# Routed feed-forward on one core: the transposes of the products moved behind the down projection

## What is computed

```python
x = x + attention(layernorm(x))            # degree-4 polynomial attention
x = x + ffn(layernorm(x))                  # routed feed-forward
x = x + silu(convolution(layernorm(x)))    # over the tokens, few taps matter
x = x + ffn(layernorm(x))                  # the same weights again

def ffn(x):   # 16 experts of width 176, 6 for a token; a shared one of width 352
    shared = (silu(x @ sg.T) * (x @ su.T)) @ shared_w2.T
    p = softmax(x @ gate_w.T); w, chosen = top_k(p, 6)
    return shared + sum(w[e] * ((silu(x @ w1g[e].T) * (x @ w1u[e].T)) @ w2[e].T) for e in chosen)
```

## Time and profile before

| | |
|---|---|
| median of 3 runs | 2374.47 us (2369.16 to 2383.44) |
| time of the profiled execution | 2393.97 us |
| its span in the trace | 2392.2 us |
| busy: PE, DVE, ACT, POOL | 2024.0, 1398.8, 1202.7, 1098.4 us |
| granted TensorE clock, mean | 0.907 of full speed |
| attention | about the first 720 us of the span |
| feed-forward and the rest | about 748 to 2320 us of the span |

### The profile page before, as it was taken

How to read it: one execution, slowest core, us unless ns; L and a number is a source line. 1 busy time by engine, 2 the same in 40 slices (tenths; PEclk the granted TensorE clock), 3 DMA queues, 4 the chain that set the end, 5 groups by cost and what they waited for, 6 DMA issues and landing times.

```text
span 2392.2 us, 42920 instructions
## 1 busy us (share of the span) xinstructions
PE 2024.0 (85%) x11630; PEld 1384.2 (58%) x11630; DVE 1398.8 (58%) x4050; ACT 1202.7 (50%) x2924; POOL 1098.4 (46%) x1235
## 2 busy tenths in 40 slices
PE   5678998998886786999988989988888999999970
PEld 3334444544434564777766767756556777677650
DVE  3556777766875664433478543587775336634643
ACT  2446665655753453455544545545444555455440
POOL 1324444444661167772453057553557717205616
PEclk8778898889878898999999999999989999999995
DMA  3174466422406433564663246653534647537743
GB/s 101 32 192 98 141 184 173 93 79 52 88 10 154 133 117 136 202 222 153 190 192 105 83 158 222 213 175 122 154 133 170 217 151 235 179 120 218 228 137 108
DMA packets 266875, 350.91 MB, mean 147 GB/s; under 512 B 55456, under 2 KB 234976, under 8 KB 265952
## 3 DMA queue, kind: packets, MB, share of 16 engines
q1 hardware_dynamic: 229792, 247.46, 36.0%
q0 software_dynamic: 36864, 100.71, 12.9%
HBM read 189.42 MB, written 167.64 MB: 149 GB/s over the span
## 4 chain that ended last, share of the span: by engine, by line
PE 42%; DVE 17%; issue 4%; POOL 4%; ACT 2%; SPq 1%; DMA 1%; POOLq 0%; DVEq 0%; ACTq 0%
PE ffn_psum L1433 22%; PE ffn_psum L1461 11%; PE ffn_psum L1441 5%; PE ffn_psum L1409 4%; DVE acc L1313 3%; DVE ysh_sb L1313 3%; POOL rows L1084 2%; POOL xs L1070 2%; DVE ac L1231 2%; DVE al L1235 1%; DVE ac L1230 1%; ACT sg L1108 1%; DVE f_stats L1205 1%; DVE xn L1326 1%; DVE lag L1325 1%
## 5 line engine op out<-in xcount | busy, mean ns | idle before, releaser
L1433 PE MATMUL ffn_psum<-w,xt 128*128 (+1 forms) x2152 | 750.8, 471 | 19.6 <-issue 19.5
L1084 POOL DMA_INDIRECT rows<-ys,idx x384 | 375.9, 979 | 418.4 <-DMA ys<-yo 286.0
L1230 DVE TENSOR_TENSOR ac<-sg,ffn_psum 128x64 f32<-128x64 f32 x602 | 130.4, 217 | 590.2 <-ACT sg L1108 587.3
L1108 ACT ACTIVATE sg<-ffn_psum 128x176 f32<-128x176 f32 x602 | 191.2, 318 | 560.2 <-PE ffn_psum L1433 560.2
L1433 PEld LDWEIGHTS ffn_psum<-w,xt 128*128 128x128 f32 x2152 | 377.3, 194 | 153.4 <-issue 39.7
L1461 PE MATMUL ffn_psum<-wd,ah 128*128 (+1 forms) x1806 | 446.3, 316 | 0.2 <-DVE al L1235 0.2
L440 DVE TENSOR_TENSOR a<-a 128x1024 f32<-128x1024 f32 (+2 forms) x304 | 326.1, 1097 | 125.3 <-ACT a L343 124.8
L343 ACT ACTIVATE a<-attn_psum 128x1024 f32<-128x1024 f32 (+1 forms) x320 | 290.8, 941 | 161.2 <-PE attn_psum L654 160.8
L1070 POOL DMA_INDIRECT xs<-xn,idx x288 | 282.9, 982 | 156.4 <-issue 86.2
L1441 PEld LDWEIGHTS ffn_psum<-f_ident,ac 128*128 128x128 f32 x1204 | 164.9, 144 | 308.7 <-DVE ac L1231 173.5
L1441 PE MATMUL ffn_psum<-f_ident,ac 128*128 128x128 f32 x1204 | 242.5, 284 | 113.9 <-DVE ac L1231 113.7
(11 more groups left out here) (178 smaller groups left out, 2363.7 us busy)
## 6 DMA issues: line engine op xcount, KB each, us to landing
xin<-xs SPq DMA_DIRECT2D x474, 128.0 KB
ys<-yo SPq DMA_DIRECT2D x474, 128.0 KB
acc<-x SPq DMA_DIRECT2D x24, 512.0 KB, 4.6
xs<-x SPq DMA_DIRECT2D x3, 2944.0 KB, 12.2
qt<-sq SPq DMA_DIRECT2D x128, 64.0 KB, 2.3
kt<-sq SPq DMA_DIRECT2D x128, 64.0 KB, 2.3
ysh<-yo SPq DMA_DIRECT2D x64, 128.0 KB
ysh_sb<-ysh SPq DMA_DIRECT2D x16, 512.0 KB, 6.0
```

The source lines that it names most:

```text
L1084: pool.indirect_dma_start(rowset(q, b)[:, k, :], None, ys[g % 3][0:NBK[g] * P, :], bass.IndirectOffsetOnAxis(at, 0)).then_inc(s_rows[j % 4 ...
L1108: act.activation(sg[:, n % 2], GU(n)[:, 0:IH], ACT.Silu).then_inc(s["sg"], 1)
L1433: last = pe.matmul(GU(n)[:, 0:wide], x[:, k * P:(k + 1) * P], of(k), start=k == 0, stop=k == KE - 1)
```

## The change

On PE, `transpose_act(n-1)` moves from behind `gate_up(n)` to the end of the round, behind `down(n-2)`. On ACT, `high_act(n-1)` moves from behind `silu(n)` to behind `output(n-2)`, so that ACT meets the PE steps in the new order. Nothing is added or removed; DVE, POOL and SP keep their lists. The line numbers below are those of the kernel before, which the order of the calls alone changes.

```diff
@@ ACT
                 if 0 <= n < NI:
                     silu(n)
-                if 0 <= n - 1 < NI:
-                    high_act(n - 1)
                 if 0 <= n + 2 < NI and own_x(n + 2):
                     high(n + 2)
...
                 if 0 <= n - 2 < NI and closes(n - 2):
                     output(n - 2)
+                if 0 <= n - 1 < NI:
+                    high_act(n - 1)
@@ PE
                 if 0 <= n < NI:
                     gate_up(n)
-                if 0 <= n - 1 < NI:
-                    transpose_act(n - 1)
                 if 0 <= n + 2 < NI and own_x(n + 2):
                     transpose_rows(n + 2)
                 if 0 <= n - 2 < NI:
                     down(n - 2)
+                if 0 <= n - 1 < NI:
+                    transpose_act(n - 1)
```

## The result

| | before | after |
|---|---|---|
| median | 2378.09 us (4 runs, 2369.16 to 2383.44) | 2502.18 us (4 runs, 2494.55 to 2511.72) |
| profiled execution, its span | 2393.97, 2392.2 us | 2503.97, 2502.2 us |
| granted TensorE clock, mean | 0.907 | 0.920 |

The ratio is 1.0528 (95% interval 1.0476 to 1.0579): slower by 5.3%, 124 us by the medians and 110 us by the two spans. The forecast was 2522 us.

The account below looks back on a forecast made before the run. PE bounds the kernel, its steps back to back at 2.22 us a routed round. The terms 95 + 4 + 43 + 5 = 147 us, added to 2374.5, gave 2522 us; 2440 to 2575 for 8 in 10, own range 2480 to 2565.

Parts of the forecast that it names:

- step 2: DVE's other work starts 0.79 us later: +4 us for 22 `add_rows`, +43 us for 78 other waits.
- Step 1, the ring: Routed rounds: `gate_up` through late `al` and PE's sequencer to a later `gate_up`; 2.42 us for 2.22, +95 us.
- the extra step: PE's sequencer: one more register step for the waits of `transpose_act`, 0.15 us in the two-round path.
- the 0.10 of the sum: PE, routed rounds: a `gate_up` whose weights come late loses 0.10 us in the two-round path.
- The 0.64 us of room: Undisturbed routed round before the change: `al` plus sequencer take 3.80 us, the `gate_up` behind starts at 4.44.
- ring is dearer: Rival: slow TENSOR_LOADs decide, or the clock falls in longer rounds; 2.57 us a round, 2592 us, chance 0.10.
- ring is hidden: Rival: PE's sequencer gets ahead of the wait, rounds stay at 2.22; +80, so 2455 us, chance 0.20.
- "+43": 78 waits near shared items, each priced at 0.55 us, the middle between 0.20 and 0.91; bounds 16 and 71 us.
- Step 3, the removed wait: PE: the 113.7 us of `transpose_act` waits for the product nearly vanish but aren't gained; `down` meets the same delay.
- Step 4, the clock: PE's granted clock: longer waits in dense stretches may bring a few more drops, +5 us, between 0 and 25.
- The signs asked for: Traces: 2.42 us rounds, "issue" before `gate_up` some hundreds of times, `down` waiting for `al`, `al` at 3.31 to 3.33 us.
- faster: Rival: short product waits vanish with the "issue" behind them; up to 133 us gained, half expected, 2314 us, chance 0.04.

Follow-up runs that it names:

- the early read: Read of the expert's number moved one round earlier, ahead of the wait for `al`: kernel before 2348.15 us, changed kernel 2423.69 us.
- a second read: Expert's number read twice for each routed item: changed kernel 3265.3 us, ratio 1.0721; kernel before 3141.56 us, ratio 1.033.
- ACT's half: Kernel before with only `high_act(n-1)` moved behind `output(n-2)`, PE's order kept: 3120.28 us, ratio 1.0335, and 2512.75 us, ratio 1.0559.
- the transposes in the middle: Kernel before with `transpose_act(n-1)` between `transpose_rows(n+2)` and `down(n-2)`, `high_act(n-1)` between `high(n+2)` and `output`: 2385.57 us, ratio 1.0024.
- the undisturbed comparison: Follow-up runs with their own runs of the kernel before, which took 2380.45 us (13 runs), as in the result.
- the long one: Follow-up runs in which engines stood still for 1 to 50 us at a time; the kernel before took 3011.05 us, in another such set 3041.77 us.

## Why the prediction came out right, and where it was off

Slower was right, and so was the main mechanism; the amount was 2522 against 2502 us, inside the range. That it came so near is in part luck: the price of a ring round was too low, and the rounds that pay it and the price of step 2 were too high.

**Step 1, the ring.** Shown. The best of the rounds came as it was worked out: `high_act` 0.29 behind `output` (0.29), `al` at 3.31 (3.33), `al` to the next load 1.39 and 1.43 (1.41 with the extra step). The `gate_up` of that 3.31 had its weights in time and took 1.35 us; where they come late it takes 1.45, and `al` comes at 3.41, as in 69 of the 91 rounds. So the 0.10 of the sum was right as well. But the windows give 2.47 us a round, not 2.42. Most of the difference is that I took a median where a ring pays for every slow read. Over the 91 clean rounds the reads are (ns min/median/max), in the changed kernel and then in the one before:

```profile
L1423 PEldq TENSOR_LOAD <-table x91: 295/307/762, 979.8 to 1202.5; - x91
```

```profile
L1423 PEldq TENSOR_LOAD <-table x91: 296/302/537, 979.4 to 1179.7; - x91
```

By the records of each round the mean of a read in the changed kernel is 0.38 us, one in eight is over 0.60, and from the end of `al` to the second `gate_up` it is 1.56 us on the mean (1.39 to 1.91); `al` itself comes at 3.39 on the mean (3.31 to 3.42). 3.39 + 1.56 = 4.95 for two rounds, 2.47 for one. Of the 0.21 over the best rounds' 4.74, the reads themselves are 0.08, the later `al` 0.08 (the late weights, which the sum had), and the rest comes behind the read. Before, the reads were quicker (0.32 on the mean, none over 0.54) and off the path: all rounds but one took 2.22, that one 2.32. Why some reads are slow, and more of them in the changed kernel, was not tried.

The other factor, 474 rounds, was too high. By the table of rounds above the ring is paid in 378 of them, 0.22 on the mean: 82 us, where the sum had 95. Far from any longer round it is 0.25, next to one 0.17.

That the ring needs the read is shown by the early read (2.22 again); that the read's time lies in it, by the leg behind `al` with a second read (2.10 in place of 1.56) and by the two runs of ACT's half; that it needs a late `al`, by the transposes in the middle. The 0.64 us of room before holds for a later `al` only; for more steps of the sequencer it is 0.27.

The Trainium skill's rule in "Advanced Engine Details and Errata", section Sequencer and Instruction Queues, that an engine instruction may wait in a queue while the sequencer reads on, did not save this kernel, whose wait stands on a register step; its other rule there, that the sequencer itself does the control instructions, is what the run with the second read agrees with (2.61 us a round with PE waiting for no one).

The reads themselves, in the changed kernel (ns min/median/max):

```profile
L1423 PEldq TENSOR_LOAD <-table x474: 295/302/932, 947.8 to 2422.8; - x158
```

The median is that of the earlier trace rows. The rival *ring is dearer* (2.57 a round) had half a case: slow reads in a part of the rounds do act, with a third of the price that it gave them (2.47 against 2.42 and 2.57). The floor of about 600 ns of the Trainium skill, "DMA: Bandwidth & Descriptors", section Latency and other measured facts, does not hold for these reads either: most are half of it.

**Step 2, other DVE work.** Over-priced. The prediction charged the ring in all 474 routed rounds and 4 + 43 = 47 us on top. In the stretch with 11 `add_rows`, (109.1 - 39 x 2.47) / 11 = 1.16 us each, where the earlier trace rows gave 1.17 before and I had 1.37. The first shared stretch, which has no reads and hence no ring, took 204.6 against 201.0 us: +3.6 us (for one `high_act` less within its bounds), where 15 to 20 waits at up to 0.91 were feared. By the table of rounds the 95 long routed rounds cost +24 us and the 128 shared ones +7. Of the 24 the prediction had 95 x 0.20 = 19 in step 1; so 24 + 7 - 19 = 12 us stand where it had 47.

The mechanism itself exists: with the ring off, the same lateness costs 0.95 us for an `add_rows`, 53 us in the long routed rounds, and 64 to 75 us in all, which is near the +80 of the rival *ring is hidden*. What was wrong is "+43", the 78 waits at the middle between 0.20 and 0.91. The kernel before paid 30 us in its long rounds for reads behind a wait and the changed one 1 us, and this the prediction left out. I had let one loss cover the other for `add_rows` and not for the remaining 78.

**Step 3, the removed wait.** Shown: 113.7 us gone from `transpose_act`, 152.3 us come to `down`. Nothing was gained.

**Step 4, the clock.** Wrong in sign, small in size. The two stretches of the earlier trace rows have a granted clock of 0.90 and 0.96 now, against 0.88 and 0.95, and the mean rose from 0.907 to 0.920. The longer waits did not bring more time at half speed, they came with less. What that is worth was not measured by itself; it looks like a few us. Up to the first read, 946.0 before and 947.8 now, only 1.8 us were lost, with the first shared stretch costing 3.6 of its own and starting 4.4 us earlier than before (744.20 against 748.60), though nothing ahead of it was changed.

**The signs asked for.** "Issue" before `gate_up` "some hundreds of times": PE's list has 106, because a gap shorter than the modelled end of the matmul before it does not count there. The list of the weight loads has it:

```profile
PEld ffn_psum L1433 <- issue: 106.5, 307, 0.9
```

307 times, and 106.5 us. Before it was 101 times and 41.8 us, so 65 us more, a large part of the ring's 82. In the prediction the 54 marks on PE were said to come "behind each such stall"; there are 100 stalls, and the list of the loads has 101 marks. The other signs came: 2.47 where 2.42 was asked, 0.29, 3.31 for 3.33, and below 1.4 us an `add_rows`.

The sum, then: +82 in the short routed rounds, +24 in the long ones, +7 in the shared ones, 113 between the first and the last `gate_up`; the first came 4.5 us earlier, and the spans differ by 110. In the prediction's own accounting the ring is 82 + 19 = 101 us for 95, step 2 is 12 for 47, and the clock, not worked out apart, had +5. The total was off by 37 us in the profiled execution (2541 against 2504).

Two figures of the prediction don't follow from its own terms. The range of 2480 to 2565 is narrower than the bounds of steps 1, 2 and 4 added up: 36 + 4 + 16 + 0 = 56 and 213 + 4 + 71 + 25 = 313 us, or 2430 to 2688. And the rival *faster* at half of 133 us would be at 2308, not 2314.

## What to carry to other kernels

When you move a step to the end of a loop, look for what reads a register behind a wait: a value that PE's sequencer must load before it can address the next weights makes a wait that looks free (`al` is in time for `down`) into a ring over two rounds. Take such reads out from behind the waits first: done alone it made the kernel before 1.5% faster (2348 against 2380 us, interval 0.9 to 2.1%), the fastest kernel of the undisturbed comparison. In the long one the same edit gave 0.2%, at the edge of the noise, so its worth depends on what else holds the kernel up. And do not add the prices of two delays that lie in the same round: ask for each what it costs when the other is there, set the two traces against each other round by round, and look at the weight loads' list, not only at the matmuls', for gaps of a few tenths of a microsecond.

## What the runs showed of the hardware

- PE's sequencer can be the bound by itself: with a second read of 0.65 us a round went from 2.22 to 2.61 us, and in that stretch PE's list has no wait for another engine.
- In the changed kernel it took 1.39 to 1.91 us in the clean rounds from the end of `al`, for which a register step waits, to the `gate_up` behind it; the load of the value alone took 0.30 at best and 0.76 at worst. In the kernel before, bound by PE's matmuls, reads of 0.30 to 0.54 us left almost every round at 2.22; in the ring the spread is paid for.
- In two of the three comparisons engines stood still for long times. ACT in the kernel before with the early read, timeline; "remote" is a releaser that the trace doesn't hold:

```profile
1340.01 0.32 ACT L1108 ACTIVATE sg<-ffn_psum 128x176 f32<-128x176 f32 x1 [3.14 <-remote]
...
1354.07 0.38 ACT L1121 ACTIVATE yo<-ffn_psum 128x256 f32<-128x256 f32 x1 [8.73 <-remote]
...
1361.77 0.32 ACT L1108 ACTIVATE sg<-ffn_psum 128x176 f32<-128x176 f32 x1 [7.32 <-remote]
```

The kernel before was 631 and 661 us longer in these two. What caused the holes stays open. The record gives another chip for each of the three comparisons, so chip and time of the run can't be told apart. The rounds between the holes ran at nearly the pace of the undisturbed runs: 2.22 with the early read in both, 2.46 against 2.50 for ACT's half.
